# A recommendation tower on Trainium2: tail buffers on shared places, and a tenth one-hot table in three of eight blocks

## The chip, the cores and the metric

The kernel runs on one core of one Trainium2 chip. The metric is the device time of one execution in microseconds (us). Engines: PE is TensorE (PEld its weight loads), DVE is VectorE, ACT is ScalarE, POOL is GpSimd, SP is SyncE, which here only issues DMAs.

## The reference

A batch of 2048 samples has 26 integer ids and 128 dense numbers each. Every id picks a row of 128 floats from its table (seven tables of 1000 rows, ten of 1250, eight of 12500, one of 125000). The 26 rows and the dense vector are multiplied with each other in pairs, and the 351 products go with the dense vector through three layers:

```python
e = jnp.stack([tbl_0[ids[:, 0]], ..., tbl_25[ids[:, 25]]], axis=1)
combined = jnp.concatenate([e, r_dense_x[:, None, :]], axis=1)        # 27 x 128
interact = jnp.einsum('bfd,bgd->bfg', combined, combined)
z = interact[:, _TRIU_I, _TRIU_J]                                      # 351 pairs
h = jnp.concatenate([z, r_dense_x], axis=1)                            # 479
h = jnp.maximum(h @ W_top1 + b_top1, 0.0)                              # 512
h = jnp.maximum(h @ W_top2 + b_top2, 0.0)                              # 256
y = h @ W_top3
```

All of it is float32.

## The kernel before, in words

The batch is cut into 8 blocks of 256 samples, numbered 0 to 7, and each block into two tiles of 128. What has to be built for each block is `xt`: for every sample the 27 vectors, with the 128 numbers on the partitions.

There are two ways in which a table's rows get there. **Gathered**: POOL issues one indirect DMA per table and tile (line 615), which brings 128 rows into `raw`; PE turns them over (`turn_rows`, line 632), three or four tables into one PSUM bank; ACT copies the bank to `xt` (line 858). `raw` has two places, so tile t + 2 overwrites tile t. **One-hot**: the smallest tables are kept in SBUF whole, split into a rounded part `hot_hi` and a remainder `hot_lo`. The ids of a block, broadcast to all partitions (`ids_wide`, loaded by SP), are compared on DVE with row numbers, which gives a matrix of zeros and ones (`make_piece`, line 909). A piece is this for up to four chunks of 128 rows, and DVE is at most three pieces ahead of PE (`RING`). PE multiplies table and matrix, two matmuls for each chunk, hi and lo (`hot_piece`, line 651), and ACT copies the result (line 401). A table in a block is called an item. Before the change 9 tables are one-hot in every block (seven of 8 chunks, two of 10) and 17 are gathered. In block 0 five of the one-hot tables are used as they were loaded, in full float32, before they are split.

Then come, for each tile, the products: 4 samples at a time, two PSUM fills of 128 small matmuls (`products`, line 670), which ACT copies to `gram` (line 423). Behind the second tile of a block comes its tail: four "cols" steps turn `gram` over (line 699) and ACT copies the pairs into `z` (lines 437 to 446); two "zt" steps turn `z` over (line 704), with a rounded part and a remainder, `zt_hi` and `zt_lo`; four "h1" and two "h2" steps are the layers (line 726), `h1_hi`, `h1`, `h1_lo` and `h2` their results, and "y" is the last one (line 682). The dense vector enters `xt` and the first layer; for the latter it is split too: ACT rounds `dense_sb` to `dense_hi` (line 836, behind the copy of an item in the middle of the block), DVE writes the remainder `dense_lo` (line 497, at the step "cols" 0). PE's use of both is in "h1". The last block has no later work beside its tail and has a sequence of its own, which begins with `last_start` (lines 740 and 744).

The order of the work is written out once, as a list of steps in slots, for PE, ACT and DVE alike (lines 176 to 240): the items of block h + 1 stand between the products and the tail of block h, the turns of a tile are put behind ends of items (`with_turn`), and the tail steps are spread over the slots by a table of covers. Each engine walks the same list and does its own part, in order. The items that PE works on while the products of block h run are those of block h + 1, and the turns that follow are those of tiles 2h + 1 and 2h + 2. PE fills three PSUM banks for turns and items in rotation (`x_ps`); a fill waits until ACT has copied the fill three before it.

SP issues the loads in its own order: ids, the one-hot tables (two halves each, two halves at once), the dense blocks and the weights. Where it waits, all loads behind it wait. Before the change one load of ids holds four items, and there are two places for them.

`SHARES` gives, for each block, how many of the one-hot tables are gathered there all the same; before the change it is zero for all, and the branch of the slot list for blocks with a share is not taken. The lines that matter:

```python
if SHARES[h + 1] == 0:
    slots += with_turn(rest_slots, t + tiles_block, ends)
else:
    slots += with_turn(slots[-1:] + rest_slots, t + tiles_block, [0] + [end + 1 for end in ends[:-1]])[1:]
```

In a block with a share the turns of the first tile stand one item earlier in the list than in a block without one.

Of the kernel before, what the change touches and what calls it, by code (L numbers as in the profile page):

```python
# [6 lines left out]
F32 = mybir.dt.float32  # L7
F32R = mybir.dt.float32r
# [4 lines left out]
P = 128  # L13
BLOCK = 256
SLOTS = 32
QUAD = 4
FILLS = 2
BANK = 512
HOT = 9
DIRECT = 5  # L20
SHARES = (0,) * 8
# [3 lines left out]
DENSE = 2  # L25
# [12 lines left out]
IDS = 4  # L38
# [5 lines left out]
def block_orders(nh):  # L44

    first = list(range(MOST, nh)) + list(range(MOST))
    once = [j for j in first if j < min(SHARES[1:])]
    direct = [j for j in first if j in first[:2 * DIRECT:2] or j in once]
    return first, [j for j in first if j not in direct] + direct, direct
# [11 lines left out]
def build(nc, dense_t, ids, hot_ids, tables, hot_tables, w1, b1, w2, b2, w3, out):  # L61
# [206 lines left out]
    with ExitStack() as ctx:  # L268
# [14 lines left out]
        dense_sb = [sb(f"dense_sb{k}", [P, BLOCK]) for k in range(DENSE)]  # L283
        dense_hi = [sb(f"dense_hi{k}", [P, BLOCK], F32R) for k in range(DENSE)]
        dense_lo = [sb(f"dense_lo{k}", [P, BLOCK], F32R) for k in range(DENSE)]
# [13 lines left out]
        z = sb("z", [P, QUAD, z_wide])  # L299
        h2 = sb("h2", [P, m2, BLOCK])  # L300
        zt_hi = sb("zt_hi", [P, n_kz, BLOCK], F32R)
        zt_lo = sb("zt_lo", [P, n_kz, BLOCK], F32R)
        h1_hi = sb("h1_hi", [P, m1, BLOCK], F32R)
        with nc.sbuf_tensor("h1", [P, m1, BLOCK], F32) as h1:
            pass
# [158 lines left out]

        def tail_copy(act, h, key):
# [5 lines left out]
            if kind == "cols":  # L471
                last = pairs_copy(copy, j)
            elif kind == "zt":
                for src, hi in zt_parts(j, ps, zt_hi):
                    last = copy(hi, src)  # L475
                last.then_inc(zt_rounded, 1)
                return
            elif kind == "h1":
                bias = b1_sb[:, j:j + 1]
                nc.scalar.activation(h1_hi[:, j, :], ps[:, 0:BLOCK], ACT.Relu, bias=bias).then_inc(h1_rounded, 1)  # L480
                last = nc.scalar.activation(h1[:, j, :], ps[:, 0:BLOCK], ACT.Relu, bias=bias)  # L481
            elif kind == "h2":
                last = nc.scalar.activation(h2[:, j, :], ps[:, 0:BLOCK], ACT.Relu, bias=b2_sb[:, j:j + 1])
            else:
                y_copy(act, h, ps)
                act.sem_inc(tail_copied[bank], 1)
                y_store(act, h)
                return
# [6 lines left out]
        def dense_residue(dve, h):  # L495
            dve.wait_ge(dense_rounded, h + 1)
            nc.vector.tensor_tensor(dense_lo[h % DENSE][:, :], dense_sb[h % DENSE][:, :],
                                    dense_hi[h % DENSE][:, :].bitcast(F32), ALU.subtract).then_inc(dense_split, 1)
# [122 lines left out]
        def _(pe):  # L621
# [64 lines left out]
            def tail_step(h, key, part):  # L686
# [18 lines left out]
                elif kind in layer:  # L705
                    products_of = layer[kind]
                    w = slice(j * P, (j + 1) * P)
                    for n in range(cuts[kind][part], cuts[kind][part + 1]):
# [8 lines left out]
                        if b[0] == "x":  # L717
                            weights = {"hi": w1z_hi, "lo": w1z_lo}[a][:, k, w]
                            moving = {"x hi": dense_hi, "x lo": dense_lo}[b][h % DENSE][:, :]
# [19 lines left out]
            def last_start(m):  # L739
                nc.tensor.matmul(last_h1[m], ident[:, :], b1_sb[:, m:m + 1].to_broadcast([P, BLOCK]), start=True, stop=False)  # L740
                for weights, part in ((w1z_hi, dense_hi), (w1z_lo, dense_hi), (w1z_hi, dense_lo)):
                    if m == 0:
                        pe.wait_ge(dense_rounded if part is dense_hi else dense_split, h + 1)
                    nc.tensor.matmul(last_h1[m], weights[:, n_kz, of[m]], part[h % DENSE][:, :], start=False, stop=False)  # L744
# [73 lines left out]
        def _(act):  # L818
# [8 lines left out]
            def hot_copy(it):  # L827
# [4 lines left out]
                if it == (it - j_th[it] + last_item[first] + 1) // 2:  # L832
# [3 lines left out]
                    copy(dense_hi[h % DENSE][:, :], dense_sb[h % DENSE][:, :]).then_inc(dense_rounded, 1)  # L836
# [7 lines left out]
            for kind, *what in order:  # L844
# [14 lines left out]
                elif kind == "tail":  # L859
                    h, key, part = what  # L860
                    if part == parts[key] - 1:
                        tail_copy(act, h, key)
                elif kind == "gram":
# [146 lines left out]
```

## Time and profile before

| | |
|---|---|
| median of 3 runs | 377.03 us (376.68 to 377.2) |
| profiled execution | 377.81 us |
| its span, first to last instruction | 375.9 us |
| granted TensorE clock, mean of the span | 0.999 |
| PE busy, weight loads busy | 344.1 us, 319.9 us |
| POOL busy, DVE busy, ACT busy | 266.5, 225.2, 180.4 us |
| moved by DMA | 31.23 MB, 83 GB/s over the span |

The time of an execution is its span and some 1.9 us around it. A busy time is what the profiler counts as execution: matmuls overlap and their ends are modelled, so a matmul's own duration is longer than the distance from its start to the next one's. In a list of groups a row has busy time and mean duration of one, then the idle time of the engine just before them and what ended it. "issue" stands for time in which the engine waited for nothing that the profile shows.

### The profile page before, as it was taken

How to read it: one execution, taken by the hardware profiler on the slowest of the kernel's cores; microseconds unless marked ns; L12 is line 12 of the kernel's file. 1: busy time of each engine (PE TensorE's matmuls, PEld its weight loads, DVE VectorE, ACT ScalarE, POOL GpSimd, SP SyncE). 2: the span in 40 equal slices, each digit the busy share in tenths (PEclk: the TensorE clock that was granted, in tenths of full speed). 3: DMA queues.
4: the chain of work that ended last, by engine and by line, in shares of the span. 5: the costliest groups of instructions: out<-in, count | busy, mean ns of one | idle time of the engine just before them, and what ended most of it. 6: DMA issues, size and time to landing. Idle time of an engine off the chain costs nothing.

```text
span 375.9 us, 14417 instructions
## 1 busy us (share of the span) xinstructions
PE 344.1 (92%) x6464; PEld 319.9 (85%) x6464; DVE 225.2 (60%) x256; ACT 180.4 (48%) x475; POOL 266.5 (71%) x280
## 2 busy tenths in 40 slices
PE   2987979999999999999999988999999999998786
PEld 1776878989989999999989988999989988988776
DVE  5696798955468634874469543775469543722132
ACT  2345445374535554473536453473636553464432
POOL 6777787777777777777777777777777777777300
PEclk9999999999999999999999999999999999999999
DMA  5778424232222323222222323132232232212100
GB/s 176 231 205 254 126 72 112 75 85 80 68 78 57 85 68 83 57 70 64 71 82 58 81 65 86 54 84 82 69 78 60 65 87 52 60 51 59 30 3 0
DMA packets 17612, 31.23 MB, mean 83 GB/s; under 512 B 5776, under 2 KB 8720, under 8 KB 17552
## 3 DMA queue, kind: packets, MB, share of 16 engines
q0 software_dynamic: 8704, 17.84, 18.7%
q1 hardware_dynamic: 7920, 11.68, 10.6%
q8 instruction: 51, 0.84, 0.9%
q10 hardware_dynamic: 928, 0.80, 0.7%
q14 instruction: 9, 0.07, 0.1%
HBM read 30.29 MB, written 0.01 MB: 81 GB/s over the span
## 4 chain that ended last, share of the span: by engine, by line
POOL 60%; issue 25%; DMA 8%; PE 4%; ACT 1%; POOLq 0%; DVE 0%
POOL raw L615 60%; DMA raw<-in_tbl,ids_sb 8%; PE gram_ps L670 1%; PE x_ps L767 1%; DMA ids_sb<-in_ids 1%; PE tail_ps L778 1%; PE tail_ps L699 0%; PE x_ps L744 0%; PE x_ps L771 0%; POOLq L268 0%; PE tail_ps L704 0%; PE x_ps L740 0%; PE tail_ps L784 0%; PE row_ps L767 0%; ACT xt L858 0%
## 5 line engine op out<-in xcount | busy, mean ns | idle before, releaser
L615 POOL DMA_INDIRECT raw<-in_tbl,ids_sb x272 | 265.6, 977 | 84.1 <-issue 79.5
L909 DVE TENSOR_TENSOR onehot<-ids_wide,row_ps 128x1024 fp32r<-128x1024 int16 (+1 forms) x160 | 179.0, 1162 | 57.9 <-PE x_ps L651 55.4
L651 PE MATMUL x_ps<-onehot,hot_hi 128*128 128x256 f32 x566 | 145.0, 292 | 5.5 <-DVE onehot L909 1.6
L651 PE MATMUL x_ps<-onehot,hot_lo 128*128 128x256 f32 x566 | 139.1, 281 | 0.4 <-issue 0.4
L651 PEld LDWEIGHTS x_ps<-onehot,hot_hi 128*128 128x128 f32 x566 | 106.5, 188 | 8.7 <-ACT xt L401 3.3
L651 PEld LDWEIGHTS x_ps<-onehot,hot_lo 128*128 128x128 f32 x566 | 106.7, 189 | 1.1 <-issue 1.1
L401 ACT COPY xt<-x_ps 128x256 f32<-128x256 f32 x72 | 49.1, 682 | 74.4 <-PE x_ps L651 74.3
L670 PE MATMUL gram_ps<-xt 128*27 128x26 f32 x4096 | 54.9, 192 | 5.4 <-ACT xt L858 1.2
L670 PEld LDWEIGHTS gram_ps<-xt 128*27 128x27 f32 x4096 | 45.5, 104 | 14.9 <-issue 8.0
L858 ACT COPY xt<-x_ps 128x384 f32<-128x384 f32 (+1 forms) x80 | 44.6, 623 | 3.8 <-PE x_ps L632 3.8
L632 PE MATMUL x_ps<-ident,raw 128*128 128x128 f32 x272 | 39.3, 277 | 6.0 <-DMA raw<-in_tbl,ids_sb 2.3
L423 ACT COPY gram<-gram_ps 128x416 f32<-128x416 f32 (+1 forms) x32 | 16.2, 507 | 54.2 <-PE gram_ps L670 53.5
L632 PEld LDWEIGHTS x_ps<-ident,raw 128*128 128x128 f32 x272 | 30.2, 140 | 10.7 <-ACT xt L401 5.4
L514 DVE TENSOR_TENSOR h_lo<-h,h_hi 128x256 fp32r<-128x256 f32 x28 | 11.9, 425 | 41.2 <-ACT h L481 41.2
L651 PE MATMUL x_ps<-onehot,hot_in 128*128 128x256 f32 x84 | 20.8, 404 | 7.8 <-DMA hot_in<-in_tbl 7.2
L651 PEld LDWEIGHTS x_ps<-onehot,hot_in 128*128 128x128 f32 x84 | 16.6, 203 | 10.9 <-issue 7.5
L508 DVE TENSOR_TENSOR zt_lo<-tail_ps,zt_hi 128x512 fp32r<-128x512 f32 (+2 forms) x24 | 12.3, 512 | 18.5 <-ACT zt_hi L475 16.6
L726 PE MATMUL tail_ps<-zt_hi,weights_lo 128*128 128x256 f32 (+1 forms) x84 | 21.6, 283 | 0.0
L726 PE MATMUL tail_ps<-zt_hi,weights_hi 128*128 128x256 f32 (+1 forms) x84 | 21.6, 284 | 0.0
L825 ACT CAST hot_hi<-hot_in 128x1024 fp32r<-128x1024 f32 (+1 forms) x9 | 9.9, 1095 | 21.6 <-DMA hot_in<-in_tbl 21.6
L480 ACT ACTIVATE h_hi<-tail_ps,b_sb 128x256 fp32r<-128x256 f32 x28 | 13.5, 481 | 9.0 <-PE tail_ps L726 8.9
L699 PE MATMUL tail_ps<-ident,gram 128*128 128x128 f32 x104 | 16.2, 274 | 1.6 <-ACT gram L423 0.7
(93 smaller groups left out, 336.3 us busy)
## 6 DMA issues: line engine op xcount, KB each, us to landing
raw<-in_tbl,ids_sb POOLq DMA_INDIRECT x272, 2.6
ids_wide<-in_hot_ids SPq DMA_DIRECT2D x17, 256.0 KB
hot_in<-in_tbl SPq DMA_DIRECT2D x14, 256.0 KB, 3.4
weights_in_place<-in_w SPq DMA_DIRECT2D x12, 128.0 KB, 2.4
hot_in<-in_tbl SPq DMA_DIRECT2D x4, 320.0 KB, 4.3
dense_sb<-in_dense_t ACTq DMA_DIRECT2D x6, 128.0 KB, 2.4
dense_sb<-in_dense_t SPq DMA_DIRECT2D x2, 128.0 KB, 3.1
ids_wide<-in_hot_ids SPq DMA_DIRECT2D x1, 192.0 KB
```

Of the source, the lines that this page charges most:

```text
L401: last = copy(xt[:, place:place + (b - a) * P, feature], src[:, a * P:b * P])
L423: copy(gram[rows, :, per_fill * i:per_fill * (i + 1)], src).then_inc(done, 1)
L480: nc.scalar.activation(h1_hi[:, j, :], ps[:, 0:BLOCK], ACT.Relu, bias=bias).then_inc(h1_rounded, 1)
L508: last = nc.vector.tensor_tensor(lo, src, hi.bitcast(F32), ALU.subtract)
L615: nc.gpsimd.indirect_dma_start(out=raw[k][:, f, :], out_offset=None, in_=sources[f], in_offset=bass.IndirectOffsetOnAxis(ap=ids_sb[:, t, f ...
L632: last = nc.tensor.transpose(ps[:, c * P:(c + 1) * P], raw[k][:, f, :], ident[:, :])
L651: last = nc.tensor.matmul(ps, table[:, chunk_at[j] + c, :], moving[:, c - a, :], start=(c == 0 and table is tables_of[0]), stop=(c == chun ...
L670: last = nc.tensor.matmul(gram_ps[m % 2][SLOTS * s:SLOTS * s + feats, cols], xt[:, b, 0:feats], xt[:, b, 0:feats - 1], start=True, stop=True)
L699: last = nc.tensor.transpose(ps[:, c * P:(c + 1) * P], gram[:, q:q + 2, :].rearrange("p q g -> p (q g)"), ident[:, :])
L726: last = nc.tensor.matmul(ps[:, 0:BLOCK], weights, moving, start=(n == 0), stop=(n == len(products_of) - 1))
L858: copy(xt[:, b:b + P, fs[0]:fs[-1] + 1], src).then_inc(x_copied, 1)
L909: nc.vector.tensor_tensor(columns(p), ids_wide[:, it // IDS % IDS_RING, it % IDS, 0:width].unsqueeze(1).to_broadcast([P, n, width]), row_n ...
```

## The change

The constant `HOT` goes from 9 to 10 and `SHARES` from all zero to one for blocks 0, 1, 3, 5 and 7. The tenth table is one of 1250 rows (10 chunks). It is loaded behind the other nine, it is gathered in the five blocks with a share, 17 gathers a tile as before, and it is a one-hot item, the last of its block, in blocks 2, 4 and 6, which have 16 gathers a tile (four turns of four in place of 3, 3, 4, 3 and 4). Blocks 3, 5 and 7 take the other branch of the slot list above.

The room for it in SBUF comes from buffers put on one place: `dense_lo` on `dense_sb`, `zt_lo` on `h2`, and `z` with `h1` and `h1_lo`, which had one place already; `dense_hi` has one place in place of two, and a load of ids holds three items in place of four (25 loads in place of 18). Since `dense_hi` has one place, ACT rounds into it later: at "cols" 0 of the block's tail, ahead of the copies of that step, and for the last block at the step "start", behind the copy of the products before it. DVE's remainder waits for this rounding, as it did before.

The core of the diff:

```diff
-HOT = 9
+HOT = 10
 DIRECT = 5
-SHARES = (0,) * 8
+SHARES = (1, 1, 0, 1, 0, 1, 0, 1)
...
-IDS = 4
+IDS = 3
...
-    return first, [j for j in first if j not in direct] + direct, direct
+    late = [j for j in first if j < SHARES[0]]
+    return first, [j for j in first if j not in direct + late] + direct + late, direct
...
-        dense_sb = [sb(f"dense_sb{k}", [P, BLOCK]) for k in range(DENSE)]
-        dense_hi = [sb(f"dense_hi{k}", [P, BLOCK], F32R) for k in range(DENSE)]
-        dense_lo = [sb(f"dense_lo{k}", [P, BLOCK], F32R) for k in range(DENSE)]
+        dense_sb, dense_lo = [], []
+        for k in range(DENSE):
+            with nc.sbuf_tensor(f"dense_sb{k}", [P, BLOCK], F32) as loaded:
+                dense_sb.append(loaded)
+            dense_lo.append(sb(f"dense_lo{k}", [P, BLOCK], F32R))
+        dense_hi = sb("dense_hi", [P, BLOCK], F32R)
...
-        z = sb("z", [P, QUAD, z_wide])
-        h2 = sb("h2", [P, m2, BLOCK])
         zt_hi = sb("zt_hi", [P, n_kz, BLOCK], F32R)
+        with nc.sbuf_tensor("h2", [P, m2, BLOCK], F32) as h2:
+            pass
         zt_lo = sb("zt_lo", [P, n_kz, BLOCK], F32R)
         h1_hi = sb("h1_hi", [P, m1, BLOCK], F32R)
+        with nc.sbuf_tensor("z", [P, QUAD, z_wide], F32) as z:
+            pass
         with nc.sbuf_tensor("h1", [P, m1, BLOCK], F32) as h1:
             pass
         h1_lo = sb("h1_lo", [P, m1, BLOCK], F32R)
...
+        def dense_round(h):
+            nc.scalar.copy(dense_hi[:, :], dense_sb[h % DENSE][:, :]).then_inc(dense_rounded, 1)
+
         def tail_copy(act, h, key):
...
             if kind == "cols":
+                if j == 0 and h < blocks - 1:
+                    dense_round(h)
                 last = pairs_copy(copy, j)
...
                     to_xt(copy, first, tiles_block, nf + nh, dense_sb[h % DENSE]).then_inc(dense_copied, 1)
-                    copy(dense_hi[h % DENSE][:, :], dense_sb[h % DENSE][:, :]).then_inc(dense_rounded, 1)
...
+                elif kind == "start" and what == [0]:
+                    dense_round(blocks - 1)
```

The uses of `dense_hi` and `dense_lo` on DVE and PE follow; nothing else changes.

## Rows read from the trace of the kernel before

**Rows 1.** The page, busy time (share of the span) and instructions of each engine.

```profile
PE 344.1 (92%) x6464; PEld 319.9 (85%) x6464; DVE 225.2 (60%) x256; ACT 180.4 (48%) x475; POOL 266.5 (71%) x280
```

**Rows 2.** The page, the chain that ended last, by engine.

```profile
POOL 60%; issue 25%; DMA 8%; PE 4%; ACT 1%; POOLq 0%; DVE 0%
```

**Rows 3.** The page, costliest groups: busy, mean ns of one, idle before.

```profile
L615 POOL DMA_INDIRECT raw<-in_tbl,ids_sb x272 | 265.6, 977 | 84.1 <-issue 79.5
```

**Rows 4.** Timeline of POOL, the last two gathers: start, duration, instruction, idle before.

```profile
349.17 0.96 POOL L615 DMA_INDIRECT raw<-in_tbl,ids_sb  x1 [0.30 <-issue]
350.43 0.94 POOL L615 DMA_INDIRECT raw<-in_tbl,ids_sb  x1 [0.30 <-issue]
```

**Rows 5.** Busy time by stretch, 95 to 354 us.

```profile
core 0: us, PE busy (x) PEld busy (x) DVE busy (x) ACT busy (x) POOL busy (x), PEclk, DMA share, GB/s
95.00:354.00 259.00, 248.73 (x4872) 235.25 (x4870) 148.63 (x164) 130.35 (x363) 194.31 (x204) 1.00 0.26 69
```

**Rows 6.** Timeline of POOL, last gather of the second tile, blocks 2, 3, 4, 6.

```profile
136.75 0.95 POOL L615 DMA_INDIRECT raw<-in_tbl,ids_sb  x1 [0.30 <-issue]
...
179.53 0.95 POOL L615 DMA_INDIRECT raw<-in_tbl,ids_sb  x1 [0.30 <-issue]
...
222.50 1.08 POOL L615 DMA_INDIRECT raw<-in_tbl,ids_sb  x1 [0.30 <-issue]
...
307.82 1.05 POOL L615 DMA_INDIRECT raw<-in_tbl,ids_sb  x1 [0.30 <-issue]
```

**Rows 7.** Timeline of PE, last transposes of the same tiles, and of block 7.

```profile
140.83 0.60 PE L632 MATMUL x_ps<-ident,raw 128*128 128x128 f32 x2
...
182.47 0.30 PE L632 MATMUL x_ps<-ident,raw 128*128 128x128 f32 x1
...
225.16 0.41 PE L632 MATMUL x_ps<-ident,raw 128*128 128x128 f32 x2 [1.08 <-ACT xt L858]
...
310.52 0.30 PE L632 MATMUL x_ps<-ident,raw 128*128 128x128 f32 x1 [1.14 <-DMA raw<-in_tbl,ids_sb]
...
353.08 0.30 PE L632 MATMUL x_ps<-ident,raw 128*128 128x128 f32 x1 [1.20 <-DMA raw<-in_tbl,ids_sb]
```

**Rows 8.** The tile raw, its gathers from issue to landing.

```profile
DMA to landing us min/median/max: 2.4/2.6/4.7
```

**Rows 9.** Timeline of PE: one-hot matmuls, transposes and what follows them.

```profile
149.80 0.28 PE L651 MATMUL x_ps<-onehot,hot_lo 128*128 128x256 f32 x1
...
151.96 0.28 PE L651 MATMUL x_ps<-onehot,hot_lo 128*128 128x256 f32 x1
...
164.62 0.37 PE L651 MATMUL x_ps<-onehot,hot_hi 128*128 128x256 f32 x1
164.82 0.28 PE L651 MATMUL x_ps<-onehot,hot_lo 128*128 128x256 f32 x1
...
204.90 1.58 PE L632 MATMUL x_ps<-ident,raw 128*128 128x128 f32 x11
206.32 0.27 PE L699 MATMUL tail_ps<-ident,gram 128*128 128x128 f32 x1
```

**Rows 10.** Timeline of PE, in the middle of an item.

```profile
234.64 0.28 PE L651 MATMUL x_ps<-onehot,hot_hi 128*128 128x256 f32 x1 [1.02 <-issue]
```

**Rows 11.** The tile dense_hi: durations in ns (min/median/max), first and last start.

```profile
L836 ACT CAST dense_hi<-dense_sb x8: 440/456/469, 30.6 to 322.0; 128x256 fp32r<-128x256 f32 x8
L497 DVE TENSOR_TENSOR dense_lo<-dense_sb,dense_hi x8: 415/418/473, 78.2 to 356.6; 128x256 fp32r<-128x256 f32 x8
```

**Rows 12.** Timeline of ACT, from "cols" 0 of block 2 to the next item's copy.

```profile
158.49 0.49 ACT L442 COPY z<-tail_ps 64x100 f32<-64x100 f32 x2 [0.70 <-PE tail_ps L699]
...
159.44 0.69 ACT L401 COPY xt<-x_ps 128x256 f32<-128x256 f32 x1
```

**Rows 13.** Timeline of DVE: a table's remainder in block 0, the dense remainder of block 2.

```profile
33.79 1.49 DVE L895 TENSOR_TENSOR hot_lo<-hot_in,hot_hi 128x1280 fp32r<-128x1280 f32 x1 [2.96 <-ACT hot_hi L825]
...
159.24 0.47 DVE L497 TENSOR_TENSOR dense_lo<-dense_sb,dense_hi 128x256 fp32r<-128x256 f32 x1
```

**Rows 14.** Timeline of ACT and DVE, copies of the last block's products.

```profile
355.95 0.50 ACT L423 COPY gram<-gram_ps 64x416 f32<-64x416 f32 x1 [1.47 <-PE gram_ps L670]
355.95 0.59 DVE L423 COPY gram<-gram_ps 64x416 f32<-64x416 f32 x1 [6.71 <-PE gram_ps L670]
```

**Rows 15.** Timeline of PE, last_start.

```profile
357.06 0.39 PE L744 MATMUL x_ps<-dense_lo,weights_hi 128*128 128x256 f32 x1 [0.29 <-DVE dense_lo L497]
```

**Rows 16.** The list of groups, one-hot pieces on DVE.

```profile
L909 DVE TENSOR_TENSOR onehot<-ids_wide,row_ps 128x1024 fp32r<-128x1024 int16 (+1 forms) x160 | 179.0, 1162 | 57.9 <-PE x_ps L651 55.4 <-DVE zt_lo L508 0.9 <-DMA ids_wide<-in_hot_ids 0.8
```

**Rows 17.** Waits of DVE for ids: us in total, times, longest.

```profile
DVE onehot L909 <- DMA ids_wide<-in_hot_ids: 0.8, 1, 0.8
```

**Rows 18.** Timeline of ACT, the ninth table's rounding and the copies after it.

```profile
37.43 1.26 ACT L825 CAST hot_hi<-hot_in 128x1280 fp32r<-128x1280 f32 x1 [2.71 <-DMA hot_in<-in_tbl]
...
44.44 0.68 ACT L401 COPY xt<-x_ps 128x256 f32<-128x256 f32 x1 [3.75 <-PE x_ps L651]
```

More of the change, by code:

```diff
@@ L497, in dense_residue @@
             nc.vector.tensor_tensor(dense_lo[h % DENSE][:, :], dense_sb[h % DENSE][:, :],
-                                    dense_hi[h % DENSE][:, :].bitcast(F32), ALU.subtract).then_inc(dense_split, 1)
+                                    dense_hi[:, :].bitcast(F32), ALU.subtract).then_inc(dense_split, 1)
         def tail_split(dve, h, key):
@@ L718, in tail_step @@
                             weights = {"hi": w1z_hi, "lo": w1z_lo}[a][:, k, w]
-                            moving = {"x hi": dense_hi, "x lo": dense_lo}[b][h % DENSE][:, :]
+                            moving = {"x hi": dense_hi, "x lo": dense_lo[h % DENSE]}[b][:, :]
                         elif kind == "h1":
@@ L740, in last_start @@
                 nc.tensor.matmul(last_h1[m], ident[:, :], b1_sb[:, m:m + 1].to_broadcast([P, BLOCK]), start=True, stop=False)
-                for weights, part in ((w1z_hi, dense_hi), (w1z_lo, dense_hi), (w1z_hi, dense_lo)):
+                for weights, part in ((w1z_hi, dense_hi), (w1z_lo, dense_hi), (w1z_hi, dense_lo[h % DENSE])):
                     if m == 0:
                         pe.wait_ge(dense_rounded if part is dense_hi else dense_split, h + 1)
-                    nc.tensor.matmul(last_h1[m], weights[:, n_kz, of[m]], part[h % DENSE][:, :], start=False, stop=False)
+                    nc.tensor.matmul(last_h1[m], weights[:, n_kz, of[m]], part[:, :], start=False, stop=False)
             pe.wait_ge(ident_ready, 1)
```

## The prediction

> **What bounds the kernel now.** I read the page first: TensorE (PE) 92% busy, its weight loads 85%, POOL 71%, DVE 60%, ACT 48% [rows 1]. By that alone PE is the bound. The chain that ended last says another thing: 60% of it is POOL and 25% is issue time [rows 2], both the one line that issues the gathers, 272 of them [rows 3]. The reader is to see there that POOL is not "71% busy with 29% to spare": one gather starts 1.25 us after the one before it (349.17 to 350.43), of which the row counts 0.95 as busy and 0.30 as issue [rows 4], and it does so through the whole kernel, to the last gather at 350.43. POOL runs without a break, 34 gathers a block, 42.5 us a block.
>
> So two engines are nearly full, and the question is by how much PE is the quicker. From 95 to 354 us PE is busy for 248.7 of 259.0 us [rows 5], so it is idle for 10.3. I look next at where PE meets the gathers: the last group of transposes of the second tile of each block. The last gather of that tile starts at 136.75, 179.53, 222.50, 307.82 and 350.43 in blocks 2, 3, 4, 6 and 7 [rows 4, 6]; the transposes start (after those of the group before, which share a row in the first one) at about 141.1, then at 182.47, 225.16, 310.52 and 353.08 [rows 7]. The distances are 4.3, 2.9, 2.66, 2.70 and 2.65 us. A gather lands 2.6 us after its issue in the median, 2.4 at the least [rows 8]. So PE came from behind, caught POOL in block 4, and from there on it waits for a landing about once a block: 1.08, 1.14 and 1.20 us [rows 7], 3.4 us together. (The first is put down to an ACT copy, the distance of 2.66 us says it is the landing.) That is all that late gathers cost PE, and all that a quicker POOL can give back: up to block 3 PE was behind POOL, not ahead of it.
>
> **The change part by part.** The sum is made against the profiled execution: 377.81 us, span 375.9 and 1.9 around it. The median of the runs is 377.03, 0.8 lower; I add the sum to the median.
>
> *Six gathers fewer.* Blocks 2, 4 and 6 gather 16 rows a tile in place of 17: 6 x 1.25 = 7.5 us less on POOL, whose last gather would start near 342.9. On the end this is worth only the 3.4 us of PE waits above: **-3.4**.
>
> *A tenth one-hot item in blocks 2, 4 and 6.* The table has 1250 rows, 10 chunks, hi and lo: 20 matmuls, 60 in all. In a run of 19 of them the starts go from 149.80 to 151.96, 0.12 us each [rows 9], though a row says 0.28: they overlap. 60 x 0.12 = **+7.2**. The first matmul of an item takes 0.20 to the next (164.62 to 164.82 [rows 9]), 0.08 more: **+0.2**. Out go 6 transposes: 11 of them last from 204.90 to 206.32 [rows 9], 0.13 each: **-0.8**. All of this is in PE's own queue, in order, and nothing hides it unless PE would have waited there.
>
> *One interruption that belongs to no work.* In the middle of an item PE stood for 1.0 us and waited for no semaphore [rows 10]. It may or may not return; I take half: **-0.5**.
>
> *The dense rounding moves* from the copy of a one-hot item to the first "cols" step of the tail, on ACT, 0.456 us [rows 11]. In blocks 3, 5 and 7 the three last groups of transposes now follow at once on the item behind that step, and the third needs the PSUM bank of this item, whose copy stands behind the rounding and the z copies in ACT's queue. In the trace of before such a copy began at 159.44, 0.95 after the first z copy at 158.49 [rows 12]: it would be just in time without the rounding, and up to 0.45 late with it. Bounds 0 and 0.45 a block; I take 0.3, nearer the upper one since ACT has only 0.70 idle before those copies: **+0.9**. In even blocks the copies that PE needs next stand ahead of the rounding: 0.
>
> DVE gets a wait: the dense residue now needs this rounding, and one-hot pieces are queued behind it, for which PE waits. In the trace DVE came to the residue at 159.24 [rows 13], 0.75 after ACT was free for the tail, so the rounding (0.45) would have been over; cost 0. Without that cover it is up to 0.45 for each of 7 blocks, 3.2.
>
> *At the end* the last block's rounding sits behind the gram copy, in line with the residue. ACT ends that copy at 356.45, DVE its half at 356.54 [rows 14]; then 0.456 and 0.418 [rows 11] and two hand-overs of some 0.05 give 357.4, where PE now goes on at 357.06 [rows 15]. This is on the path: **+0.4**.
>
> *At nothing:* the nine extra DVE pieces (1.16 us each, where DVE waits 55 us for PE [rows 16]) and the tenth table's residue, 1.5 us once as for the other table of that size [rows 13]; if neither were covered, 1.5 once. The loads of ids by three: in the trace DVE waits for ids once, 0.8 us, at the start [rows 17]; SP meets a few more waits, and behind it only weights are queued, which are needed much later. The tenth table's load on SP, ahead of the weights: ACT will wait for it as it did for the ninth (2.71 and a cast of 1.26), but then it idles 3.75 us for PE [rows 18]; uncovered it is 1.3. Buffers that share a place bring no other wait that I find: the tail's order on PE already separates their uses.
>
> **Sum:** -3.4 + 7.2 + 0.2 - 0.8 - 0.5 + 0.9 + 0.4 = +4.0; 377.0 + 4.0 = **381.0 us**. POOL then has some 11 us to spare at its last landing (342.9 + 2.65 against PE at 353.1 + 3.6), and PE is the only bound.
>
> On judging room on PE, the trace and a rule differ. The trace: starts 0.12 us apart, weight loads of 0.19 that overlap them, and 10.3 us idle in 259. The Trainium skill, "Perfetto Trace Analysis", section "Identifying the Most-Contended Engine", says that matmul busy time is a poor measure of PE's headroom and that the busy share of the weight loads is a good one. By that rule's 85% PE could take the 60 matmuls, and the sum would keep POOL's term alone.
>
> **Rivals.**
> A, *PE has the room, POOL stays the bound*: the end follows the last gather, -7.5 + 0.4, or 369.9 us. For it: the chain of waits names POOL [rows 2], weight loads are 85% [rows 1]. Against it: +6.6 us of PE work would have to go into 10.3 us of idle time, only 3.4 of which is a wait for gathers; the rest lies in pieces of 0.1 to 1 us at hand-overs. It decides where PE still waits for the landing of tile 15. Chance 0.07.
> B, *part of the idle time is filled*: the longer tail cover and fewer turns (8 groups in place of 10 in a block) save hand-overs. If half of the other 6.9 us goes, 377.6; if all, 374.1. For it: PE's gain on POOL differs from block to block, 1.4 us from block 2 to 3. Chance 0.19: 0.10 faster, 0.09 within 0.2% (0.75 us, about what a measurement of this kernel can tell from no change).
> C, *the rounding blocks DVE*, uncovered as above: 381.0 + 3.2 = 384.2. It decides where PE waits for one-hot pieces behind the first "cols" step. Chance 0.08.
> That the change does not do what it says I rule out by the diff: the shares give 32 gathers to blocks 2, 4 and 6, 34 to the others.
> My forecast, *PE becomes the bound*: 0.66.
>
> **The numbers.** Faster 0.07 + 0.10 = 0.17; same 0.09; slower 0.66 + 0.08 = 0.74. The forecast's own range: 378.6 (no interruption, no rounding cost, 1 us filled) to 382.8 (interruption stays, the start uncovered by 1.3). For 8 in 10 it has to reach into B and C: 376.0 to 383.5 leaves out A (0.07), the lower part of B (0.05) and the upper part of C (0.06).
>
> **What would show it.** Right: 266 gathers, the last one near 343; PE at that tile's last transposes some 13 us behind the issue, no PE wait for a landing after 95 us; PE's idle time from 95 to its last transposes about 7 us; the chain led by PE, not POOL; PE waiting about 0.8 us for the dense rounding at the end. Wrong: PE still 2.65 us behind the last gather (A), an idle time of 4 us or less there (B), or one-hot waits of PE after "cols" (C).

## The result and the profile after

The changed kernel takes 381.38 us in the median of 4 runs (380.32 to 385.29), the kernel before 376.86 in the 4 runs beside them (376.04 to 377.2). The ratio is 1.0147, 95% interval 1.012 to 1.0174. It is slower, as forecast; 381.0 was predicted, and the range of 376.0 to 383.5 holds the median. On another chip, later, the ratio was 1.0175 (1.0137 to 1.0214). Ratios are made from the single runs and not from the medians; the quotient of the two medians here is 1.012, the lower end of the interval. One slow run each of kernels 3 and 8 below (379.62 and 386.12 us) is left out of their medians and ratios.

The profiled execution of after took 380.32 us, its span is 378.3. It was the fastest of its four, while that of before (377.81) was above all four of its runs. So the two traces lie 2.5 us apart, where the medians lie 4.5 apart; this matters below.

From the page of after: the busy line, the chain by engine, and two of the costliest groups (busy, mean ns of one | idle before, releaser):

```profile
PE 350.5 (93%) x6518; PEld 326.8 (86%) x6518; DVE 235.7 (62%) x266; ACT 184.7 (49%) x473; POOL 258.4 (68%) x274
...
PE 79%; DMA 8%; ACT 5%; DVE 5%; issue 2%; SPq 0%; DVEq 0%; ACTq 0%
...
L626 POOL DMA_INDIRECT raw<-in_tbl,ids_sb x266 | 257.5, 968 | 82.3 <-issue 79.2
...
L643 PE MATMUL x_ps<-ident,raw 128*128 128x128 f32 x266 | 37.8, 276 | 1.6 <-ACT xt L407 1.6
```

The shares of busy time have hardly moved against [rows 1], PE from 92 to 93%. The chain has turned over: POOL led it with 60% and 25% of issue [rows 2], now PE does with 79% and POOL is not in it. The last line says why. Among the waits of the transposes only copies by ACT are left; the landings of raw, which stood in [rows 7], are gone from what they wait for.

How far PE is from POOL can be read at the end of the gathers. POOL's timeline, the last gather, and PE's, the last transposes:

```profile
340.50 0.94 POOL L626 DMA_INDIRECT raw<-in_tbl,ids_sb  x1 [0.30 <-issue]
```

```profile
355.26 0.93 PE L643 MATMUL x_ps<-ident,raw 128*128 128x128 f32 x7
```

Seven transposes stand in one row; the last four are tile 15's last group and start at about 355.6, 15.1 us behind the last gather, where [rows 4, 7] had 2.65. About 13 was forecast, with the last gather near 343: POOL was earlier than that by 2.4 us, of which 1.4 had arisen by tile 3 (its last gather at 92.6, before at 94.0).

The next view is busy time by stretch, from the end of tile 3's last transposes to the end of tile 15's (before: 99.5 and 353.7 us; after: 99.8 and 356.2). Columns: stretch, its length, then busy time (and instructions) of PE, PEld, DVE, ACT and POOL, granted clock, DMA share, GB/s. First before, then after:

```profile
99.50:353.70 254.20, 243.93 (x4825) 230.84 (x4827) 145.09 (x160) 126.23 (x354) 190.93 (x201) 1.00 0.26 69
```

```profile
99.80:356.20 256.40, 249.43 (x4880) 237.45 (x4883) 155.69 (x170) 129.22 (x351) 182.86 (x193) 1.00 0.27 67
```

PE's busy time has grown by 5.5 us and its idle time has shrunk from 10.27 to 6.97, 3.3 less (about 7 us of idle time were forecast). From the end of tile 15's transposes to the end of the span it is 22.2 and 22.1 us: 2.2 of the 2.4 us between the two spans arise in this stretch.

The late rounding shows where it was expected. Timelines of after, ACT and PE, in block 3, at "cols" 0 of block 2's tail and the three groups of transposes behind the item:

```profile
162.63 0.41 ACT L472 CAST dense_hi<-dense_sb 128x256 fp32r<-128x256 f32 x1 [0.93 <-PE tail_ps L710]
...
163.39 0.93 PE L643 MATMUL x_ps<-ident,raw 128*128 128x128 f32 x7
...
163.86 0.68 ACT L407 COPY xt<-x_ps 128x256 f32<-128x256 f32 x1
...
164.59 0.66 PE L643 MATMUL x_ps<-ident,raw 128*128 128x128 f32 x4 [0.28 <-ACT xt L407]
```

ACT reaches the copy of the item's bank only behind the rounding and the z copies, and the last group of transposes (the four of the last row) waits 0.28 us for that bank. The same happens in block 5 (0.29) and not in block 7, so 0.57 together.

At the end, timelines of ACT, DVE and PE in after:

```profile
358.54 0.50 ACT L429 COPY gram<-gram_ps 64x416 f32<-64x416 f32 x1 [1.56 <-PE gram_ps L681]
...
358.94 0.40 ACT L472 CAST dense_hi<-dense_sb 128x256 fp32r<-128x256 f32 x1
359.38 0.42 DVE L508 TENSOR_TENSOR dense_lo<-dense_sb,dense_hi 128x256 fp32r<-128x256 f32 x1 [0.24 <-ACT dense_hi L472]
...
359.40 0.39 PE L755 MATMUL x_ps<-dense_hi,weights_hi 128*128 128x256 f32 x1 [0.28 <-ACT dense_hi L472]
...
359.86 0.39 PE L755 MATMUL x_ps<-dense_lo,weights_hi 128*128 128x256 f32 x1
```

The third product begins 1.32 us after the copy's start; in [rows 14, 15] it was 1.11. So 0.2 us were lost here, and the unchanged 22.1 says that they came back before the end.

### The profile page after: what moved, and what is told of

Its sections match the earlier page's. It is cut to its first block, busy times and chain, and to the rows that moved or that the text cites. A ratio compares the mean times of both kernels' runs of the same rounds, so it can differ in the third digit from the quotient of the medians.

```text
span 378.3 us, 14545 instructions
## 1 busy us (share of the span) xinstructions
PE 350.5 (93%) x6518; PEld 326.8 (86%) x6518; DVE 235.7 (62%) x266; ACT 184.7 (49%) x473; POOL 258.4 (68%) x274
## 3 DMA queue, kind: packets, MB, share of 16 engines
q1 hardware_dynamic: 9216, 12.53, 11.5%
## 4 chain that ended last, share of the span: by engine, by line
PE 79%; DMA 8%; ACT 5%; DVE 5%; issue 2%; SPq 0%; DVEq 0%; ACTq 0%
PE x_ps L662 36%; PE tail_ps L737 16%; PE gram_ps L681 13%; DMA hot_in<-in_tbl 8%; PE x_ps L643 6%; DVE onehot L921 2%; PE tail_ps L710 2%; PE tail_ps L715 2%; DVE hot_lo L907 2%; ACT xt L407 2%; ACT xt L868 1%; ACT z L443 1%; PE x_ps L778 1%; PE tail_ps L693 1%; ACT z L448 1%
## 5 line engine op out<-in xcount | busy, mean ns | idle before, releaser
L626 POOL DMA_INDIRECT raw<-in_tbl,ids_sb x266 | 257.5, 968 | 82.3 <-issue 79.2
L921 DVE TENSOR_TENSOR onehot<-ids_wide,row_ps 128x1024 fp32r<-128x1024 int16 (+1 forms) x169 | 187.7, 1157 | 52.4 <-PE x_ps L662 49.8
L662 PE MATMUL x_ps<-onehot,hot_hi 128*128 128x256 f32 x596 | 152.7, 292 | 6.4 <-ACT xt L407 2.4
L662 PE MATMUL x_ps<-onehot,hot_lo 128*128 128x256 f32 x596 | 146.6, 281 | 0.3 <-issue 0.3
L662 PEld LDWEIGHTS x_ps<-onehot,hot_hi 128*128 128x128 f32 x596 | 112.2, 188 | 10.8 <-ACT xt L407 5.7
L662 PEld LDWEIGHTS x_ps<-onehot,hot_lo 128*128 128x128 f32 x596 | 112.4, 189 | 0.0
L407 ACT COPY xt<-x_ps 128x256 f32<-128x256 f32 x75 | 51.2, 682 | 65.0 <-PE x_ps L662 64.5
L868 ACT COPY xt<-x_ps 128x512 f32<-128x512 f32 (+1 forms) x74 | 44.0, 653 | 0.9 <-PE x_ps L643 0.8
L643 PE MATMUL x_ps<-ident,raw 128*128 128x128 f32 x266 | 37.8, 276 | 1.6 <-ACT xt L407 1.6
L737 PE MATMUL tail_ps<-zt_hi,weights_lo 128*128 128x256 f32 (+1 forms) x84 | 22.2, 287 | 0.0
L737 PE MATMUL tail_ps<-zt_hi,weights_hi 128*128 128x256 f32 (+1 forms) x84 | 21.8, 283 | 0.0
L907 DVE TENSOR_TENSOR hot_lo<-hot_in,hot_hi 128x1024 fp32r<-128x1024 f32 (+1 forms) x10 | 12.8, 1305 | 10.2 <-ACT hot_hi L836 10.2
```

Of the source, the lines that this page charges most:

```text
L407: last = copy(xt[:, place:place + (b - a) * P, feature], src[:, a * P:b * P])
L626: nc.gpsimd.indirect_dma_start(out=raw[k][:, f, :], out_offset=None, in_=sources[f], in_offset=bass.IndirectOffsetOnAxis(ap=ids_sb[:, t, f ...
L643: last = nc.tensor.transpose(ps[:, c * P:(c + 1) * P], raw[k][:, f, :], ident[:, :])
L662: last = nc.tensor.matmul(ps, table[:, chunk_at[j] + c, :], moving[:, c - a, :], start=(c == 0 and table is tables_of[0]), stop=(c == chun ...
L737: last = nc.tensor.matmul(ps[:, 0:BLOCK], weights, moving, start=(n == 0), stop=(n == len(products_of) - 1))
L868: copy(xt[:, b:b + P, fs[0]:fs[-1] + 1], src).then_inc(x_copied, 1)
```

## The experiments

All ratios are to the kernel before, in the runs beside them. 0.001 of a ratio is 0.38 us. Kernels 1 to 4 ran on one chip, where the kernel before took 376.42 us (21 runs), 5 to 8 on a second (377.14, 12 runs), 9 to 12 on a third (376.45, 17 runs).

| kernel | median us (range, runs) | ratio (95% interval) |
|---|---|---|
| after | 381.38 (380.32 to 385.29, 4) | 1.0147 (1.012 to 1.0174) |
| 1 tenth table's remainder left out | 378.67 (377.74 to 379.23, 5) | 1.0056 (1.0032 to 1.0079) |
| 2 the six gathers put back | 382.39 (380.65 to 384.29, 4) | 1.0148 (1.0108 to 1.0189) |
| 3 before, six gathers left out | 375.24 (373.77 to 376.76, 6) | 0.9971 (0.9944 to 0.9998) |
| 4 layout alone, nine tables | 377.97 (375.77 to 379.19, 12) | 1.0037 (1.0016 to 1.0058) |
| 5 a tenth table in block 6 alone | 380.16 (378.14 to 382.86, 4) | 1.0103 (1.0071 to 1.0134) |
| 6 in six blocks | 383.08 (382.2 to 384.42, 4) | 1.0158 (1.0134 to 1.0183) |
| 7 rounding behind the z copies | 381.31 (377.51 to 382.91, 7) | 1.0083 (1.0055 to 1.0112) |
| 8 items moved out of block 0 | 381.5 (379.69 to 384.78, 5) | 1.0127 (1.0091 to 1.0163) |
| 9 after again | 382.92 (380.2 to 385.78, 6) | 1.0175 (1.0137 to 1.0214) |
| 10 kernel 7 again | 379.99 (378.99 to 382.38, 6) | 1.0114 (1.0082 to 1.0147) |
| 11 kernel 4, rounding behind | 377.11 (375.62 to 378.34, 12) | 1.0014 (0.9998 to 1.0031) |
| 12 kernel 8, ids earlier | 380.49 (379.41 to 383.41, 6) | 1.0112 (1.0079 to 1.0145) |

Kernel 9 was expected between 1.012 and 1.017 and came out just above.

### 1. Half of the added matmuls

The matmuls of the tenth table's remainder, 10 in each of the three blocks, are left out; all else is the changed kernel's.

```diff
-                tables_of = (hot_in,) if as_loaded else (hot_hi, hot_lo)
+                tables_of = (hot_in,) if as_loaded else (hot_hi,) if j == 0 else (hot_hi, hot_lo)
```

> The changed kernel, with the tenth table multiplied by its rounded part alone: 30 of the 60 added matmuls are left out (the remainder of that table is missing from the result); gathers, pieces, copies and order stay. PE is the bound: 30 x 0.12 = 3.6 us less, 377.8 us against 381.4, and the last transposes of tile 15 some 11.5 us behind the issue of its last gather in place of 15.1. Rival (the new order, the rounding or ACT's and DVE's queues make the loss, not the matmuls): 381 us, less than 1 us gained, with new waits of PE where the matmuls were.

Measured: 1.0056 against 1.0147, 3.4 us less than after (2.3 if the medians are set against those of before). Taking work off PE shortens the kernel at once, so PE has no room. If POOL were the bound, nothing would have changed. The distance at tile 15 is 9.8 us and not 11.5, since POOL's last gather came 2.7 us later in this execution (343.24) than in after.

### 2. The six gathers put back, read by nobody

POOL issues them again behind the 16 of their tile, into the free place of raw.

```diff
+                if f == nf - 1 and gathered[t] == nf:
+                    pool.wait_ge(turn_full[k], turned(t - RAW, len(turn_groups[t - RAW]) - 1))
+                    nc.gpsimd.indirect_dma_start(
+                        out=raw[k][:, nf, :], out_offset=None, in_=sources[nf],
+                        in_offset=bass.IndirectOffsetOnAxis(ap=ids_sb[:, t, nf:nf + 1], axis=0),
+                    ).then_inc(extra_in[k], 16)
```

> The changed kernel, with the six gathers put back as work that nobody reads (into the place of the 17th row group, which is free in blocks 2, 4 and 6): POOL has 272 gathers again, PE, ACT and DVE are as in the changed kernel. PE is the bound: no change within 0.5 us of 381.4; the last gather is issued near 348.0 in place of 340.5 and PE's last transposes come 7.6 us behind it. Rival (the end follows the last gather, POOL): 7.5 us more, 388.9.

Measured: 1.0148, the same as after. The trace, POOL's last gather and PE's last transposes:

```profile
349.55 0.95 POOL L629 DMA_INDIRECT raw<-in_tbl,ids_sb  x1 [0.30 <-issue]
```

```profile
356.62 0.93 PE L652 MATMUL x_ps<-ident,raw 128*128 128x128 f32 x7
```

POOL ends 9 us later than in after and PE is still 7 us behind it. In the changed kernel these six gathers cost nothing; what was bought with the one-hot work is worth nothing there.

### 3. What the six gathers were worth before

The other half by itself: the kernel before without one gather a tile in blocks 2, 4 and 6. The transposes stay and read the row of two tiles earlier, so PE's work is the same.

```diff
-    gathers = [(t, f) for t in range(tiles) for f in range(gathered[t])]
+    gathers = [(t, f) for t in range(tiles) for f in range(gathered[t]) if not (f == nf - 1 and t // tiles_block in (2, 4, 6))]
```

> The kernel before, with six gathers left out (one gathered table in both tiles of blocks 2, 4 and 6; its transposes work on the rows of the tile two earlier, so these rows are wrong in the result) and nothing put in their place. It measures what relief of POOL is worth by itself. My theory: only PE's waits for landings come back, 3.4 us, so 373.5 against 376.9, the last gather near 343 and PE's last transposes some 6.7 us behind its issue. Rival (PE has the room that the busy share of its weight loads suggests, POOL is the bound): the whole 7.5 us, 369.4, and PE still 2.65 us behind the last gather.

Measured: 0.9971, 1.1 us, a third of what was expected. The trace, last gather, last transposes, and busy time between the same two marks as above:

```profile
340.91 0.94 POOL L615 DMA_INDIRECT raw<-in_tbl,ids_sb  x1 [0.30 <-issue]
```

```profile
350.42 0.93 PE L632 MATMUL x_ps<-ident,raw 128*128 128x128 f32 x7
```

```profile
100.20:351.30 251.10, 244.80 (x4823) 231.43 (x4825) 145.24 (x160) 125.61 (x354) 183.14 (x193) 1.00 0.26 68
```

The mechanism is right: with POOL's last gather 9.8 us ahead of the last four transposes no transpose waits for a landing, and PE's idle time falls from 10.27 to 6.30. The size is not. The spans of the two traces lie 2.3 us apart (375.9 and 373.6), the medians of the spans 1.2 (374.5 in the 21 runs of before on this chip, 373.3 in the six of kernel 3). So the profiled execution of before was a long one; that it was long by these waits is likely, by kernel 4 below, and not shown here. About 1 us (0.1 to 2.1) is what POOL cost the kernel before, and what a change to the gathers alone can win.

### 4. The layout without the tenth table

The shared buffers, the late rounding and the ids by three, with nine tables in every block and all 272 gathers.

```diff
-HOT = 10
+HOT = 9
-SHARES = (1, 1, 0, 1, 0, 1, 0, 1)
+SHARES = (0,) * 8
```

> The changed kernel's buffers, its late dense rounding and its loads of ids by three, but with nine one-hot tables in all blocks and 272 gathers, as before the change. It measures that part alone. My theory: +0.4 us at the end of the last block, where PE waits for the rounding, the rest hidden behind POOL: 377.3 against 376.9, at most 377.8. Rival (the shared places or the moved rounding carry a good part of the loss of 4.5 us): 378.5 to 381, with PE waits for z or xt copies in the middle blocks.

Measured: 1.0037, 1.4 us (0.6 to 2.2), where I gave it 0.4, or 0.9 at most. Kernel 11 below says more of where it comes from. The trace has all 272 gathers; POOL's last gather and PE's last transposes:

```profile
347.86 0.94 POOL L626 DMA_INDIRECT raw<-in_tbl,ids_sb  x1 [0.30 <-issue]
```

```profile
352.46 0.93 PE L643 MATMUL x_ps<-ident,raw 128*128 128x128 f32 x7
```

The last four transposes start 4.9 us behind the gather, in the blocks before it 5.3 to 7.0, and none waits for a landing. The gathers ended 2.6 us earlier than in the trace of before (350.43), with the same number of them. So whether POOL or PE comes last differs from one execution of 272 gathers to another, and in this one nothing of the layout's price could hide behind POOL, where I had expected all but 0.4 to hide.

### 5 and 6. One block, and six

With the tenth table in block 6 alone, and in blocks 2 to 7:

```diff
-SHARES = (1, 1, 0, 1, 0, 1, 0, 1)
+SHARES = (1, 1, 1, 1, 1, 1, 0, 1)
```

> The changed kernel with the tenth table one-hot in block 6 alone: 270 gathers, one added item. My theory by now: PE is the bound, its time without any wait for a landing is about 375.3 us (the kernel with six gathers left out), the late rounding adds about 0.5 and each added item about 1.9 (2.4 of matmuls less two transposes and two changes of group): 375.3 + 0.5 + 1.9 = 377.7 us. Rival (POOL is still the bound where one block alone is changed: two gathers less, 2.5 us): 374.

```diff
-SHARES = (1, 1, 0, 1, 0, 1, 0, 1)
+SHARES = (1, 1, 0, 0, 0, 0, 0, 0)
```

> The changed kernel with the tenth table one-hot in all of blocks 2 to 7: 260 gathers, six added items. PE is the bound: 375.3 + 0.5 + 6 x 1.9 = 387.2 us, so on one line with one block (377.7) and three (381.5). Rival (the loss comes from the uneven shares, the other branch of the slot list and the rounding, not from the items): 381 or less, since no block from 2 on has a share here.

Measured: 380.16 and 383.08; the first expectation is 2.5 us too low, the second 4.1 too high, nearer to its rival (381 or less). In the trace of the first, its fastest run, POOL sets the pace of blocks 3 to 5 as it does before (PE's last group of transposes there starts 2.9 to 3.0 us behind the last gather), and the item, in block 6, comes on top of that. By the ratio it is 3.9 us above before (2.7 to 5.1); the layout's 1.4 and the 1.7 of one item (below) make 3.1, within that interval. In the second PE is far behind POOL. Last gather, last transposes, and busy time between the two marks:

```profile
334.32 0.95 POOL L626 DMA_INDIRECT raw<-in_tbl,ids_sb  x1 [0.31 <-issue]
```

```profile
358.26 1.03 PE L643 MATMUL x_ps<-ident,raw 128*128 128x128 f32 x8
```

```profile
99.10:359.30 260.20, 254.01 (x4934) 244.47 (x4936) 164.67 (x179) 130.84 (x348) 178.73 (x188) 0.99 0.26 66
```

Put the three kernels in which PE waits for no landing in a row, by busy time of PE in that stretch: no tenth item 244.80 (kernel 3), three 249.43 (after), six 254.01. That is 4.63 for the first three and 4.58 for the next, where the prediction's terms make 6.6 for three. That the two steps are equal is chance. In kernel 6 the granted clock fell in the middle of the stretch, from 200.7 to 204.2 us, and 17 one-hot matmuls started some 0.21 us apart in place of 0.12, which is 1.5 us:

```profile
200.00:210.00 10.00, 10.00 (x74) 10.00 (x74) 7.67 (x8) 5.44 (x19) 7.56 (x9) 0.83 0.25 68
```

```profile
200.32 0.28 PE L662 MATMUL x_ps<-onehot,hot_hi 128*128 128x256 f32 x1
200.44 0.28 PE L662 MATMUL x_ps<-onehot,hot_lo 128*128 128x256 f32 x1
...
201.05 0.42 PE L662 MATMUL x_ps<-onehot,hot_lo 128*128 128x256 f32 x1
201.27 0.41 PE L662 MATMUL x_ps<-onehot,hot_hi 128*128 128x256 f32 x1
```

And the products, 3072 small matmuls in each stretch, take 41.6 us in kernel 3, 41.0 in after and 39.3 in kernel 6 (each matmul counted from its start to the next start, idle time left out); they differ as much between kernels in which they are the same work (40.7 in kernel 9, 41.9 in kernel 2).

So the item is better counted block by block, in the same way, a block going from the end of the last transposes of the block before to the end of its own. A block with nine items has 19.0 us of one-hot matmuls in kernel 3 (blocks 2, 3, 4 and 6), 4.04 of transposes of raw and 11.17 of the tail; one with ten items, at the full clock, has 21.5 (21.8 in block 2), 3.38 and 11.0 in after and in kernel 6 (blocks 2 to 6). That is +2.5, -0.66 and -0.17, together **1.7 us an item**.

Idle time in the stretch is 6.30, 6.97 and 6.19: that more work fills it does not show. Kernel 3's holds two stops without a cause in the profile (1.0 together), kernel 6's one of 1.56; after's holds the two waits of 0.57 behind the rounding.

Over whole runs the steps are not even: 0.9971, 1.0147 (kernel 9: 1.0175) and 1.0158 give 6.6 or 7.7 us from kernel 3 to after, which changes the layout too, but only 0.4 us more, or 0.6 less, from after to kernel 6. Kernel 6 has neither the waits behind the rounding nor more than 1.9 us around its span (after 2.0 to 3.4 in its ten runs), and these go some way; that its three further items cost 5 us in whole runs is not shown.

### 7 and 10. The rounding moved behind the z copies

From "cols" 0 to "cols" 3, behind its z copies, and for the last block behind the h2 copies of block 6, well before last_start.

```diff
             if kind == "cols":
-                if j == 0 and h < blocks - 1:
-                    dense_round(h)
...
+            if key == ("cols", n_cols - 1) and h < blocks - 1:
+                dense_round(h)
+            if key == ("h2", m2 - 1) and h == blocks - 2:
+                dense_round(blocks - 1)
```

> The changed kernel with the dense rounding and the remainder at the last cols step of the tail, behind its z copies, and for block 7 behind the h2 copies of block 6, so that neither stands ahead of copies for which PE waits. My theory: the waits of PE for the third turn group of blocks 3 and 5 (0.3 each) and the 0.3 at the end go, about 0.9 us less: 380.5. Rival (the rounding costs nothing, the waits have another cause): 381.4, the waits of 0.3 still there.

> The changed kernel with the dense rounding behind the z copies (and the last block's behind the h2 copies of block 6), once more beside the changed kernel on one chip. If the rounding costs PE what the trace of after shows (0.28 + 0.29 in two turns, 0.3 at the end): 0.6 to 0.9 us less than after, ratio about 1.0125. If it costs what the first comparison, made over two chips, gave (1.0147 against 1.0083): 2.4 us less.

Measured: 1.0083, and beside after on one chip 1.0114 against 1.0175, 2.3 us less by the ratios. In the trace of kernel 10 the waits are gone. The transposes from 95 us on, by line, first in after and then in kernel 10 (the last lines say what ended the idle time before them):

```profile
L643 PE MATMUL x_ps<-ident,raw x215: 270/272/328, 94.9 to 355.9; 128*128 128x128 f32 x108
its engine sat idle before it (us, times) until:
  ACT xt L407: 0.6, 2
who waited for it (us, times):
```

```profile
L645 PE MATMUL x_ps<-ident,raw x209: 270/272/328, 95.5 to 353.0; 128*128 128x128 f32 x105
its engine sat idle before it (us, times) until:
who waited for it (us, times):
```

That is 0.6 us by the trace, and at most 0.2 more at the end. The runs say 2.4 and 2.3, with intervals that nearly touch (1.0112 and 1.012) or overlap a little (1.0147 and 1.0137). The medians, each against its before, say 0.4 and 2.9. The traces do not show the rest: from tile 3 to tile 15 kernels 10 and 7 take 256.1 and 257.0 us, after and kernel 9 256.4 and 256.7. So the runs show the sign, twice; of the size the traces explain 0.6, and the rest stays open.

### 11. The same with nine tables

Kernel 4 with the rounding placed as in kernel 7.

> Nine one-hot tables in all blocks (the gathers of before), with the changed kernel's places of the buffers and ids by three, and the dense rounding behind the z copies. If the 1.4 us that the layout cost with the rounding ahead of the z copies was the rounding: equal to before, ratio 0.999 to 1.001. If it was something else of the layout (the ids by three, the places): still 1.003 to 1.004.

Measured: 1.0014 (0.9998 to 1.0031), 0.5 us, where kernel 4 had 1.4. The waits of the weight loads from 95 to 354 us (engine, what for: us in total, times, longest) have in kernel 4 a line that kernel 11 lacks:

```profile
PEld x_ps L662 <- ACT xt L407: 1.0, 5, 0.2
```

Five items start 0.2 us late, behind a bank whose copy stands behind the rounding. So 1.0 us of the layout's 1.4 is the rounding's place by the trace, and 0.9 by the ratios, though their intervals overlap. Whether the other 0.5 is anything, the interval does not say.

### 8 and 12. Trying for a faster kernel

Block 0 gathers two tables more (8 tables one-hot), which should free PE where it waits at the start, and blocks 4 and 6 take ten; the rounding is as in kernel 7. The rows of block 0's second gathered table have a place of their own.

```diff
-SHARES = (1, 1, 0, 1, 0, 1, 0, 1)
+SHARES = (2, 1, 1, 1, 0, 1, 0, 1)
...
-    first = list(range(MOST, nh)) + list(range(MOST))
+    first = list(range(MOST, nh)) + list(range(MOST))[::-1]
```

> The way the other way round at the start: as the kernel with the rounding behind, but block 0 gathers two of the ten tables (18 gathers a tile, eight one-hot items, 10 chunks less, which were used in full float32 there at 0.216 us a matmul), blocks 1, 2, 3, 5 and 7 gather one, and the tenth is one-hot in blocks 4 and 6; 270 gathers; all turns take the first branch of the slot list. My theory: PE is the bound and it is behind POOL by 20 us in block 0, so work taken from PE there counts fully: 20 x 0.216 = 4.3 less, 3.8 more in blocks 4 and 6: 375.3 - 4.3 + 3.8 = 374.8 us, below both kernels. Rival (the start is set by the arrival of the tables, not by PE's work): the 4.3 do not come back, 379 us.

Measured: 381.5, 6.7 us more than hoped. Waits of DVE and of PE (us in total, times, longest), in the trace of its slowest run (386.12):

```profile
DVE onehot L927 <- DMA ids_wide<-in_hot_ids: 11.2, 2, 10.4
```

```profile
PE x_ps L670 <- DVE onehot L927: 8.6, 3, 8.2
```

In this execution PE reached block 1's items before their ids had been loaded: these loads are triggered by the progress of the gathers, and stood in SP's queue behind weights. How long the wait was in the other runs is not known. Kernel 12 triggers the loads earlier:

```diff
-IDS_FROM = 1.8
+IDS_FROM = 2.3
```

> The kernel with eight tables one-hot in the first block and ten in blocks 4 and 6, with the ids loads triggered half a load earlier. DVE's wait of 10.4 us for ids and PE's of 8.2 us behind it go. POOL has two more gathers in the first four tiles (last issue near 96.7), so PE meets the landing there, at 99.4; from there 251.2 + 2 x 1.5 + 22.7 and 1.9 around: 378.2 us, ratio 1.003. By my earlier sum (PE gains in the first block and keeps it): 374.8.

Measured: 380.49, ratio 1.0112 against 1.0127, a difference within the intervals. In the trace the wait for ids is gone, and what PE had won, it loses at tile 3. Timelines of POOL and PE there:

```profile
96.10 0.94 POOL L634 DMA_INDIRECT raw<-in_tbl,ids_sb  x1 [0.30 <-issue]
```

```profile
98.75 0.63 PE L651 MATMUL x_ps<-ident,raw 128*128 128x128 f32 x4 [2.99 <-DMA raw<-in_tbl,ids_sb]
```

The landing, 2.65 us after the issue, decides again, as expected. My 378.2 was still 2.3 too low: I let PE run at its own pace from there, but blocks 2 and 3 gather 34 rows each, and it stays at POOL's to the end of block 3 (85.4 us for the two blocks, 83.6 in kernel 3). Neither kernel beats the one before.

## Why the prediction was right

**PE becomes the bound**: shown. Kernel 2 puts the gathers back and the time stays; kernel 1 takes matmuls away and it falls. Rival A (POOL stays the bound, 369.9) falls with these, and doubly with kernel 3: even with no work added to PE the gathers were worth 1.1 us, not 7.5. The prediction weighed a page of the Trainium skill ("Perfetto Trace Analysis", section "Identifying the Most-Contended Engine"), which judges TensorE's headroom by the busy share of its weight loads, beside the share of peak FLOPs; room could be read from 85%. In after it is 86% over the span, with PE at its limit, and in the stretch from tile 3 to tile 15 it was 91% before and is 93% after (230.84 of 254.20 us, 237.45 of 256.40). Here the measurement decides against reading room from the share of the whole span.

**-3.4 for the landings**: the mechanism is right, the size is wrong. Kernel 3 measured 1.1 (0.1 to 2.1). The waits were read from one execution, which the prediction saw to be 0.8 us above the median, and taken whole; in the trace of kernel 4, with the same 272 gathers, there is no such wait. That the excess of before's execution lay in these waits is likely and not shown.

**+7.2, +0.2 and -0.8 for the items**: 6.6 forecast, 5.1 measured block by block (three times 1.7), 4.6 as busy time of PE against kernel 3. The one-hot matmuls are as summed (7.4 forecast, three times 2.5 measured). The term that was mis-sized is the removal, costed as six transposes alone: 0.27 us an item forecast, 0.83 measured. Sixteen rows a tile go in four groups, 17 in five, so an item saves two group starts beside two transposes. The transposes take 0.66 less, of which two at 0.13 make 0.26; that the other 0.4 are the two group starts, some 0.2 each, is an estimate from this. The tail takes 0.17 less besides. The group starts are what rival B named (8 groups in place of 10); they were treated as a chance there, and are a term. The rest of rival B did not come: its sign was an idle time of 4 us or less, and 6.97 was measured.

These two errors nearly cancel: -3.4 + 6.6 = 3.2 forecast; -1.1 with 4.6 or 5.1 makes 3.5 or 4.0 measured. That the sum came so near is luck in this part.

**-0.5 for the interruption**: no stop of 1.0 us in the middle of an item returned in after between 95 and 354 us. It did in kernel 3 (0.8), so half was a fair guess.

**+0.9 for the late rounding in blocks 3, 5 and 7**: the wait is where it was put and of the size taken, 0.28 and 0.29 in blocks 3 and 5; the third does not appear, so the traces have 0.57 of the 0.9. Moving the rounding away gave 0.6 (trace) to 2.4 (ratios), so 0.9 is within what was measured and not settled by it. DVE did not wait behind it in the way of rival C: PE's waits for one-hot pieces after 95 us come to 0.2 us in after.

**+0.4 at the end**: 0.2 at the third product, and regained behind it. PE waits 0.28 us for the rounding there, where about 0.8 was the sign.

**At nothing**: the extra DVE pieces, the residue, the table's load and the ids by three. The layout's remainder of 0.5 in kernel 11, if it is one, would be theirs.

A sum from measured parts: -1.1 (kernel 3) + 4.6 (items) + 0.7 (idle time of after over kernel 3) = +4.2. The medians give 4.5, the ratio 5.5 with its interval from 4.5 to 6.6. What is missing, up to 1.3 (2.4 with kernel 9's 1.0175), is partly the time around the span (below); the rest is open. The medians of the spans alone lie 5.9 us apart for kernel 9 and its before.

## What to carry to other kernels

When two engines are nearly full, take the work off one without giving it to the other, before costing any exchange: kernel 3 shows by itself that POOL's share was worth about 1 us (0.1 to 2.1), so no trade that costs PE more than that can win. A wait in one profiled execution is a sample; set it against that execution's distance from the median, and look whether the granted clock was the same in the traces that you compare. When an edit changes how many groups a stage goes in, the group starts are a term of the sum like the instructions.

## What was not expected of the hardware

**The spread.** Before: 375.31 to 377.19 us in 17 runs; after, beside it: 380.2 to 385.78 in 6. The traces show one way for this. Up to 45 us after and kernel 10 run the same program, yet PE was busy for 33.19 and 36.30 of these us. First after, then kernel 10:

```profile
0.00:45.00 45.00, 33.19 (x171) 27.60 (x172) 31.60 (x32) 19.77 (x26) 33.23 (x40) 1.00 0.73 209
```

```profile
0.00:45.00 45.00, 36.30 (x284) 30.89 (x285) 34.32 (x34) 21.29 (x28) 33.23 (x39) 1.00 0.73 211
```

POOL did the same in both. Kernel 10 reached the end of tile 3's transposes at 97.1 us, after at 99.8, and as both take some 256 us from there to tile 15's, the head start reaches the end. Where PE waits for a landing, as kernel 12 does at tile 3, a quick start of PE ends there. This does not explain all of the spread: kernel 4, with all 272 gathers, ranged from 375.77 to 379.19 us in 12 runs, and kernel 6, with PE far behind POOL, only from 382.2 to 384.42 in 4.

**The time around the span.** 1.9 or 2.0 us in every run of kernels 4 and 11, but 2.0 to 4.0 in those of after and of kernels 7, 9 and 10, also beside kernel 11 on one chip. No row says what it is.

**The granted clock.** It fell from 1.00 to 0.83 in one ten-us slice of kernel 6 in the steady stretch (above), and in some of the first 80 us in one execution and not in another of nearly the same work. Two slices of kernel 3, then the same of after:

```profile
30.00:40.00 10.00, 9.27 (x48) 7.99 (x49) 6.59 (x8) 6.24 (x12) 7.87 (x8) 0.83 0.70 213
...
50.00:60.00 10.00, 8.05 (x168) 7.50 (x167) 10.00 (x10) 2.79 (x5) 7.87 (x8) 0.83 0.51 123
```

```profile
30.00:40.00 10.00, 8.14 (x48) 6.53 (x47) 6.82 (x7) 6.03 (x9) 7.74 (x8) 1.00 0.79 219
...
50.00:60.00 10.00, 7.89 (x174) 6.98 (x173) 10.00 (x10) 2.68 (x5) 8.16 (x7) 1.00 0.44 118
```

In kernel 3 part of each slice ran at 1.2 GHz in place of 2.4, in after none, though PE was idle for longer there. In the slice before, from 20 to 30 us, PE had been busy for 8.62 us in kernel 3 and 8.50 in after, at 1.00 in both, so these rows do not tell what made it fall. From 100 us on the clock was 1.00 in both.
